# Two cross attentions, a linear and a low-rank attention, and a mixture of experts: outer products moved to VectorE, query evictions to ScalarE, fp16 halves in the last attention's projections, another turn in the routing

## The reference

```
x = x + L0_xattn(layernorm(x), ctx)   # queries Wq, keys Wk; values are ctx itself, scores / 32
x = x + L0_attn(layernorm(x))         # causal linear attention, 64 heads of 4:
        q, k = softmax(q), softmax(k)              # over the 4 of a head
        kv = cumsum(k (outer) v); kn = cumsum(k)   # over the rows
        out = (q . kv) / (q . kn), then Wo, bo
x = x + L0_ffn(layernorm(x))          # 3 cycles of a coupling net: gelu, gelu, gelu, sigmoid; twist
x = x + L1_xattn(layernorm(x), ctx)   # scores / 16, values ctx @ Wv + bv
x = x + L1_attn(layernorm(x))         # 16 heads of rank 64, value-output matrix 256x256 a head
x = x + L1_ffn(layernorm(x))          # attention over the 2 batches (4 heads), layernorm,
        # mixture of experts: gate of 8, argmax, at most 64 rows an expert in order of arrival;
        # h = rows @ w1 + b1 (1024), y = h @ w2 + b2, times the gate; layernorm
```

## Time and profile before

| | us |
|---|---|
| median of three runs (558.95 to 559.49) | 559.3 |
| the profiled execution | 559.52 |
| its span | 557.7 |
| TensorE busy (its granted clock: 0.995 of full speed) | 517.9 |
| VectorE, ScalarE, GpSimd busy | 355.6, 283.1, 76.5 |
| first cross attention and what it needs | 0 to 161 |
| between the cross attentions | 161 to 200 |
| second cross attention | 200 to 327 |
| low-rank attention | 327 to 475 |
| last attention | 475 to 500 |
| routing and experts | 500 to 558 |

### The profile page before, as it was taken

One profiled execution on the slowest core, in us unless ns is written; L12 is line 12 of the kernel. 1 busy time (PEld: TensorE's weight loads), 2 busy tenths in 40 slices (PEclk: granted clock), 3 DMA queues, 4 the chain that ended last, 5 costly groups with the idle time before them and its releaser, 6 DMA issues.

```text
span 557.7 us, 9466 instructions
## 1 busy us (share of the span) xinstructions
PE 517.9 (93%) x3588; PEld 357.5 (64%) x3588; DVE 355.6 (64%) x848; ACT 283.1 (51%) x616; POOL 76.5 (14%) x66
## 2 busy tenths in 40 slices
PE   8799998998999998999989999899999999988992
PEld 6565664555666654657545778788888778774551
DVE  4874646964547853356465647898888777654235
ACT  3777952627732038584266836898865444021110
POOL 0124131200011100000001320233301111200001
PEclk9999999999999999999999999999999999999998
DMA  8965570000000010000330040122158005960001
GB/s 270 307 208 102 115 160 29 1 2 1 1 0 1 1 29 0 2 1 0 109 118 2 2 152 2 39 78 77 39 164 351 1 1 183 350 223 1 1 1 38
DMA packets 45198, 44.06 MB, mean 79 GB/s; under 512 B 18657, under 2 KB 41185, under 8 KB 45025
## 3 DMA queue, kind: packets, MB, share of 16 engines
q1 hardware_dynamic: 45152, 43.45, 25.3%
HBM read 38.73 MB, written 0.52 MB: 70 GB/s over the span
## 4 chain that ended last, share of the span: by engine, by line
PE 65%; DVE 17%; issue 10%; ACT 6%; POOL 1%; DMA 1%; SPq 0%; DVEq 0%; ACTq 0%; POOLq 0%
PE ps L649 10%; PE ps L678 8%; PE ps L788 7%; PE ps L804 7%; PE ps L663 4%; PE ps L680 4%; PE ps L957 3%; PE ps L773 3%; PE ps L982 3%; PE ps L710 2%; PE ps L761 2%; PE ps L876 1%; DVE mx L1547 1%; ACT arena L1135 1%; ACT arena L1120 1%
## 5 line engine op out<-in xcount | busy, mean ns | idle before, releaser
L649 PE MATMUL ps<-ctx_tr,qtl 128*128 128x512 f16 x384 | 90.7, 379 | 2.1 <-ACT arena L1135 1.4
L1547 DVE TENSOR_REDUCE mx<-arena 128x1 f32<-128x512 f32 x64 | 43.1, 682 | 35.3 <-ACT arena L1135 34.6
L649 PEld LDWEIGHTS ps<-ctx_tr,qtl 128*128 128x128 f16 x384 | 36.7, 98 | 40.8 <-issue 3.2
L1135 ACT ACTIVATE arena<-ps 128x512 f32<-128x512 f32 x64 | 37.9, 595 | 43.9 <-PE ps L649 43.8
L678 PE MATMUL ps<-ctx_nat,pth 128*128 128x512 f16 x172 | 58.4, 379 | 0.0
L1120 ACT ACTIVATE arena<-arena,small 128x512 f32<-128x512 f32 x64 | 45.8, 716 | 6.3 <-DVE small L1556 6.3
L804 PE MATMUL ps<-arena,ctx_tr 128*128 128x256 f16 x384 | 47.2, 273 | 0.1
L680 PE MATMUL ps<-ctx_nat,ptl 128*128 128x256 f16 x172 | 46.9, 273 | 0.0
L663 PE MATMUL ps<-const,arena 128*128 128x128 f32 x256 | 39.1, 275 | 5.8 <-ACT arena L1120 5.1
L1561 DVE TENSOR_TENSOR ptl<-ps,pth 128x512 f16<-128x512 f32 x43 | 29.6, 688 | 21.6 <-ACT pth L1128 21.4
L1302 POOL TENSOR_TENSOR rstd<-mv,col 128x2 f32<-128x2 f32 x13 | 9.9, 765 | 239.4 <-DVE mv L1407 239.3
(11 more groups left out here) (294 smaller groups left out, 1037.9 us busy)
## 6 DMA issues: line engine op xcount, KB each, us to landing
ctx_nat<-in_w_e SPq DMA_DIRECT2D x8, 1024.0 KB, 7.7
ctx_tr<-in_w_e SPq DMA_DIRECT2D x6, 1024.0 KB, 11.6
...
```

Source lines behind the costliest of these rows:

```text
L649: mm = pe.matmul(ps[:, n % 2, :], qtl[:, qh, d, u * P:(u + 1) * P], CT[:, t0:t0 + KT, kh, d, :], start=(i == 0 and d == 0), stop=(i == 2 a ...
L1135: act.activation(S[:, n % SRING, :], ps[:, n % 2, :], ACT.Copy).then_inc(s("score_copied"), 1)
L1547: dve.tensor_reduce(mx[:, u, c:c + 1], S[:, n % SRING, :], AX.X, ALU.max).then_inc(s("score_max"), 1)
```

## The change

- Linear attention of batch 1: the two outer products go from GpSimd to VectorE, right behind the softmax of the keys. Those of batch 0 stay.
- `project("y", 0)`: the copy of the turned queries and the bias evictions of the projected ones go from VectorE to ScalarE.
- `BETWEEN`, `SIDE_AT`, `PREP_AT`, `LAST_AT`, `FILL`, `FILL_BETWEEN`: other numbers.
- Last attention, tiles 0 to 2: `w6i` is cut into fp16 halves `w6h` (1536 elements a partition, the high half by ScalarE, the low half by VectorE), the turned latents into `x6h`, and the projections are three fp16 products instead of one fp32. Tile 3 is as before. `w6i` has a semaphore of its own.
- Routing: the rows of the first pair of experts are gathered first (columns 0 to 127, banks 2 and 3), then the others (384 columns, banks 6 and 7); the two evictions no longer wait for one another. `Sm` is turned behind `hidden(0)` (banks 4 to 7) instead of before, and its copies follow the evictions of `hidden(0)`.
- `combine(g)` does the products with the high half of all four tiles first and waits for the low half after them.

```diff
@@ -65,12 +65,12 @@
 LA_WAIT = 4
-FILL = (18, 6, 43, 0, 34)
+FILL = (21, 3, 40, 0, 31)
 FILL_TURN = 5
 LAST_AT = (
-    (49, 50, 51, 54, 55, 58, 59, 62, 70, 71,),
-    (65, 70,),
-    (43, 47, 48, 48, 50, 52, 54, 55, 55, 56, 57, 60, 62, 64, 67, 69,),
+    (49, 51, 53, 54, 55, 58, 59, 64, 69, 71,),
+    (40, 48, 57, 66, 70,),
+    (42, 44, 46, 48, 49, 52, 52, 54, 55, 55, 56, 57, 59, 64, 65, 67, 69,),
 )
@@ -118,47 +118,47 @@
-PREP_AT = [0, 1, 2, 3, 4, 5, 6, 7, 9, 13, 15, 23, 25, 28, 31]
+PREP_AT = [0, 1, 2, 3, 4, 5, 6, 7, 9, 15, 16, 23, 25, 28, 31]
         (
-            (67, 67, 69, 69, 69, 69, 70, 71, 76, 81, 84, 88, 88, 90, 92, 95, 97, 100, 102, 103, 104, 105, 105, 114, 118,
+            (66, 67, 68, 69, 69, 72, 73, 76, 77, 81, 87, 89, 89, 92, 93, 95, 97, 100, 102, 103, 104, 105, 105, 110, 114,
              120, 121, 122, 123, 127,),
-            (63, 67, 68, 68, 68, 72, 72, 73, 75, 89, 93, 93, 93, 93, 94, 94, 99, 102, 103, 105, 105, 105, 105, 114, 118,
-             120, 121, 121, 122, 123, 124,),
-            (64, 65, 65, 67, 69, 69, 69, 71, 71, 80, 81, 84, 87, 89, 91, 95, 97, 97, 99, 101, 103, 104, 105, 115, 117,
-             121, 124, 124, 125, 125,),
+            (63, 64, 68, 68, 68, 74, 75, 76, 78, 89, 93, 93, 94, 94, 96, 96, 99, 102, 104, 105, 105, 105, 105, 114, 114,
+             121, 121, 122, 122, 123, 124,),
+            (64, 65, 65, 67, 68, 72, 72, 75, 77, 80, 82, 85, 88, 89, 91, 93, 97, 97, 97, 100, 103, 104, 105, 111, 117,
+             123, 124, 124, 124, 125,),
         ),
...
         (
-            (4, 8, 11, 13, 14, 15, 17, 18, 23, 24, 25, 26, 30, 30, 32, 33, 34, 35, 40, 45, 46, 50, 51, 53, 54, 56, 57,
-             58,),
-            (3, 3, 5, 13, 14, 15, 16, 18, 23, 23, 23, 24, 24, 28, 30, 33, 34, 40, 45, 49, 52, 53, 53, 55, 59, 59, 61,
+            (3, 9, 9, 10, 13, 14, 17, 19, 23, 25, 26, 27, 29, 30, 32, 33, 35, 36, 40, 43, 44, 50, 51, 53, 54, 56, 60,
+             60,),
+            (1, 3, 5, 9, 13, 14, 17, 18, 23, 23, 24, 26, 27, 29, 31, 33, 35, 40, 44, 46, 49, 52, 52, 55, 59, 60, 62,
              62,),
-            (3, 4, 8, 10, 10, 12, 16, 18, 20, 21, 23, 24, 26, 27, 28, 30, 31, 34, 43, 45, 47, 49, 51, 53, 55, 56, 58,
-             59,),
+            (1, 4, 6, 8, 10, 10, 17, 18, 20, 21, 24, 26, 26, 28, 30, 30, 33, 34, 42, 45, 47, 49, 51, 53, 57, 60, 63,
+             63,),
         ),
...
 BETWEEN = (
-    "aayyayaaaayyyayaaayayyayya",
-    "aaaayayayyaayyayayyayaaa",
-    "yaaaayyayaayayyayayaayaaa",
+    "ayayayaaayyayaaayayayyayya",
+    "ayaaayaayyyyaaayyayyyaa",
+    "yaaaayaayyayayyayayaayaaa",
 )
@@ -179,7 +179,8 @@
-FILL_BETWEEN = {0: 8, 3: 6, 11: 52, 12: 6, 13: 16, 20: 8}
+FIRST_PAIR, OTHERS = (2, slice(0, 2 * CAP)), (6, slice(2 * CAP, E6 * CAP))
+FILL_BETWEEN = {0: 8, 3: 6, 11: 52, 12: 6, 13: 16, 20: 13}
@@ -322,6 +323,8 @@
         b1c = wts[:, 3856:3920].rearrange("p (e f) -> p e f", e=E6)
+        w6h = ctx_tr[:, 10752:12288].bitcast(F16).rearrange("p (h c n) -> p h c n", h=2, c=DC)
+        x6h = wts[:, 2048:2816].bitcast(F16).rearrange("p (h c n) -> p h c n", h=2, c=DC)
@@ -336,6 +339,7 @@
         ys = rest[:, 0:256]
+        turned_places = lambda g: ps[:, 4 + g, 0:SEQ].bitcast(F16)
             pe.wait_ge(s("m_qkv0"), n)
+        pe.wait_ge(s("w6_lo"), 1)
         for c in range(DC):
-            mm = pe.matmul(ps[:, 6, 0:cols[1] - cols[0]], x0T[:, c, t * P:(t + 1) * P], w6i[:, c, cols[0]:cols[1]],
-                           start=(c == 0), stop=(c == DC - 1))
+            for k, (xh, wh) in enumerate(((0, 0), (0, 1), (1, 0))):
+                mm = pe.matmul(ps[:, 6, 0:cols[1] - cols[0]], x6h[:, xh, c, t * P:(t + 1) * P],
+                               w6h[:, wh, c, cols[0]:cols[1]], start=(c == 0 and k == 0), stop=(c == DC - 1 and k == 2))
         mm.then_inc(s("m_qkv0_ps"), 1)
@@ -927,29 +934,33 @@
     pe.wait_ge(s("id16"), 1)
-    for t in range(NT):
-        pe.wait_ge(s("m_S"), t + 1)
-        for c in range(DC):
-            for h in range(2):
-                mm = pe.matmul(ps[:, c, :], y1[:, h, t, c * P:(c + 1) * P], Sm[:, t, :], start=(t == 0 and h == 0),
-                               stop=(t == NT - 1 and h == 1))
-            if t == NT - 1:
-                mm.then_inc(s("m_dis_ps"), 1)
-    for g in range(E6 // 2):
-        to = ps[:, 2 + g, 0:SEQ].bitcast(F16)
+    for to, cols in FIRST_PAIR, OTHERS:
         for t in range(NT):
-            mm = pe.transpose(to[:, t * P:(t + 1) * P], Sm[:, t, g * P:(g + 1) * P], id16)
-        mm.then_inc(s("m_ST_ps"), 1)
+            pe.wait_ge(s("m_S"), t + 1)
+            for c in range(DC):
+                for h in range(2):
+                    mm = pe.matmul(ps[:, to + c, cols], y1[:, h, t, c * P:(c + 1) * P], Sm[:, t, cols],
+                                   start=(t == 0 and h == 0), stop=(t == NT - 1 and h == 1), skip_group_check=True)
+                if t == NT - 1:
+                    mm.then_inc(s("m_dis_ps"), 1)
+
+    def turn_places():
+        pe.wait_ge(s("m_dis0"), 2)
+        pe.wait_ge(s("m_dis1"), 2)
+        for g in range(E6 // 2):
+            for t in range(NT):
+                mm = pe.transpose(turned_places(g)[:, t * P:(t + 1) * P], Sm[:, t, g * P:(g + 1) * P], id16)
+            mm.then_inc(s("m_ST_ps"), 1)
...
-        if g == 0:
-            pe.wait_ge(s("m_dis"), 2)
-        else:
+        if g < 2:
+            pe.wait_ge(s("m_dis0"), g + 1)
+            pe.wait_ge(s("m_dis1"), g + 1)
+        if g:
             pe.wait_ge(s("m_h"), 2 * g)
         pair = (2 * g, 2 * g + 1)
         for f in range(2):
         pe.wait_ge(s("m_h"), 2 * g + 2)
-        if g == 0:
-            pe.wait_ge(s("m_ST"), 4)
-        else:
+        if g:
             pe.wait_ge(s("m_hT"), 2 * g)
@@ -971,6 +980,8 @@
             pe.wait_ge(s("m_y"), g)
+        else:
+            pe.wait_ge(s("m_ST"), 4)
         pair = (2 * g, 2 * g + 1)
@@ -984,18 +995,19 @@
     def combine(g):
-        pe.wait_ge(s("m_y"), g + 1)
-        for b in range(B):
-            for t in (2 * b, 2 * b + 1):
-                for h in range(2):
+        for h in range(2):
+            pe.wait_ge(s("m_y_hi" if h == 0 else "m_y"), g + 1)
+            for b in range(B):
+                for t in (2 * b, 2 * b + 1):
                     mm = pe.matmul(ps[:, 6 + b, (t % 2) * D:(t % 2 + 1) * D], ST[:, g, t * P:(t + 1) * P], yy[:, g, h],
...
                                    skip_group_check=True)
-            if g == E6 // 2 - 1:
-                mm.then_inc(s("m_comb"), 1)
+                if g == E6 // 2 - 1 and h == 1:
+                    mm.then_inc(s("m_comb"), 1)
...
     hidden(0)
+    turn_places()
     for g in range(G):
@@ -1031,7 +1043,17 @@
     yield
-    yield
+    if (what, b) == ("y", 0):
+        act.wait_ge(s("xn_turned"), NORM[what, b] + 1)
+        act.activation(xnT_of(what, b), bank(side_banks(what, b)[0], a=DC), ACT.Copy).then_inc(s("xnT"), 1)
+    yield
+    if (what, b) == ("y", 0):
+        act.wait_ge(s("px_q"), k + 1)
+        act.wait_ge(s("px_qt"), k)
+        for e in range(DC):
+            q = act.activation(qT_of(what, b)[:, e, :], ps[:, side_banks(what)[1], e * SEQ:(e + 1) * SEQ], ACT.Identity,
+                               bias=C("%s_bq%d" % (what, e)))
+        q.then_inc(s("qT"), 1)
     yield
@@ -1211,7 +1233,7 @@
-    early = leave_pair(0, 6)
+    early = enter_last()
     for n in late(-1):
@@ -1231,6 +1253,22 @@
+            def enter_last():
+    def latents_hi(k, tiles, n):
+        act.wait_ge(s("xn_turned"), NORM["m", k] + 1)
+        w = len(tiles) * P
+        act.activation(x6h[:, 0, :, tiles[0] * P:tiles[0] * P + w], ps[:, n, 0:2 * w].rearrange("p (c n) -> p c n", c=DC),
+                       ACT.Copy).then_inc(s("m_x_hi"), 1)
+
+    act.wait_ge(s("w6i_in"), 16)
+    act.activation(w6h[:, 0], w6i, ACT.Copy).then_inc(s("w6_hi"), 1)
+    yield
+    latents_hi(0, (0, 1), 6)
+    yield
+    latents_hi(1, (2,), 6)
+    yield
+    yield from leave_pair(0, 6)
+
             def leave_pair(j, b_turn):
     act.activation(e8, e8, ACT.Exp).then_inc(s("m_exp8"), 1)
-    act.wait_ge(s("m_dis_ps"), 1)
-    act.activation(disT[:, 0, :], ps[:, 0, :], ACT.Copy).then_inc(s("m_dis"), 1)
-    for g in (0, 2):
+    for k, (at, cols) in enumerate((FIRST_PAIR, OTHERS)):
+        act.wait_ge(s("m_dis_ps"), 2 * k + 1)
+        act.activation(disT[:, 0, cols], ps[:, at, cols], ACT.Copy).then_inc(s("m_dis0"), 1)
+
+    def places(g):
         act.wait_ge(s("m_ST_ps"), g + 1)
-        act.activation(ST[:, g, :], ps[:, 2 + g, 0:SEQ].bitcast(F16), ACT.Copy).then_inc(s("m_ST"), 1)
+        act.activation(ST[:, g, :], turned_places(g), ACT.Copy).then_inc(s("m_ST"), 1)
+
     for g in range(E6 // 2):
@@ -1270,6 +1311,9 @@
             y_hi(g - 1)
+        else:
+            places(0)
     y_hi(E6 // 2 - 1)
             layernorm("y", 0)
+        if b:
+            continue
         pool.wait_ge(s("a_soft"), n + 1)
@@ -1425,14 +1471,16 @@
     yield
-    turned(what, b)
-    yield
-    dve.wait_ge(s("px_q"), k + 1)
```

(44 more changed lines are left out.)

19 lines of the change are left out of this document (10 added, 9 removed), and 6 rows, old and new, of the table SIDE_AT.

## The result

| us | before | after |
|---|---|---|
| median of 11 runs | 559.49 (558.95 to 560.68) | 557.47 (556.07 to 559.13) |
| profiled execution | 559.52, span 557.7 | 558.75, span 557.0 |

The ratio is 0.9956, 95% interval 0.9946 to 0.9967: 2.5 us faster on 559.49, between 1.8 and 3.0 (the two medians differ by 2.0). The forecast was 557.0 and "faster".

The account below looks back on a forecast made before the run. Bounds: TensorE in the low-rank stage, VectorE between the attentions, a relay from routing on. Terms -0.35-1.0-0.75-0.2, lists 0, sum to -2.3 on 559.52: 557.2 profiled, 557.0 median; range 555.0 to 559.0 (forecast's own 556.2 to 558.1).

Parts of the forecast that it names:

- Part 1: Between the cross attentions: the chain and the next attention's first scores come 0.35 us earlier; from -0.98 to +1.2.
- account of the stall, -1.85: Between the attentions: VectorE's twist takes 2.33 us beside GpSimd's product, 0.48 without; the move saves 1.85.
- +0.59 for them up to the queries: Between the attentions: VectorE's added outer products, 2.44, less the stall, 1.85, up to batch 0's normalised queries.
- +0.59 for the place: Between the attentions: by the shared-port rule against moving work, the place gives +0.59 us, not -0.35.
- Part 2: Low-rank stage, last attention's projections in fp16 halves: 1.94 us saved, 0.9 lost, so -1.0; from -1.94-0.4 to +0.4.
- the step that binds: Low-rank stage, step 23: VectorE's 1.75 us load minus 0.6 falls on 0.96 of slack; 0.2 to 0.8 of stall.
- the price put on top: Low-rank stage: stall up to 0.8 us at step 23 and 0.3 each at steps 24 and 25; 1.1 in all.
- rival (a): Low-rank stage: VectorE absorbs the weights' low half, TensorE gets 1.94 and the exposed loads; -1.3 more, 555.7; chance 0.20.
- Part 3: Routing: experts start at 508.0 instead of 508.75, transposes hidden; -0.75 us, from -0.9 to -0.3.
- Part 4: Last combine: four products go during the 0.52 us wait for the low half; -0.2 us, from -0.4 to 0.
- Part 5: Lists of the two cross attentions: waits move, nothing gained; 0 us, from -1.0 to +1.0.
- Rival (c): Second cross attention: the feed-forward's early Gelu delays the row maxima; up to +5 us on the forecast, 562.0; chance 0.11.

Follow-up runs that it names:

- e9: Kernel after with batch 1's outer products back on GpSimd and 8 instead of 13 dummy products ahead of the queries' turn; median 556.19 us, ratio to before 0.9942.
- e1: Kernel before with only the fp16 halves of the last attention's projections added; median 557.84 us, ratio to before 0.9982.
- e6: Kernel after with the subtraction that makes the weights' low halves done twice; median 558.61 us, ratio to before 0.9984.
- e3: Kernel before with only the routing and last-combine edits added; median 559.13 us, ratio to before 0.9997.
- e4: Kernel before with only the new lists of the two cross attentions (PREP_AT, SIDE_AT); median 559.88 us, ratio to before 1.0007.

## Why the prediction was right, and where its steps were off

| part | forecast | own trace | in after |
|---|---|---|---|
| 1 between the attentions | -0.35 | -0.37 and -0.27 later | -0.40 |
| 5 lists | 0 | +0.33 | with the -0.27: +0.02 |
| 2 halves | -1.0 | -1.85 | -1.85 |
| 3 routing | -0.75 | -0.66 | -0.67 |
| 4 combine | -0.2 | -0.22 | -0.22 |
| sum | -2.3 | -3.04 | -3.12 |

The direction and the sizes of parts 1, 3 and 4 were right. That the time came within 0.5 us of the forecast is in part luck, since two differences of opposite sign met: by the traces the edits gave 0.8 more than foreseen, and the run times show 0.6 less of it than the traces.

**Part 1** was right in size, and in what bounds it (the query product, then TensorE's sums, with VectorE waiting 0.49). Its account of the stall, -1.85, was right too. What it did not draw from its own working is that the outer products gain nothing in it: the working has +0.59 for them up to the queries, 0.4 with the gaps taken off (measured 0.29), and e9 shows 0.27 lost. The rule that moving work between these two engines might not help (the Trainium skill, Perfetto Trace Analysis, "Optimizing Scalar/DVE Operations") is borne out by that 0.27; the whole part is still a gain, so the prediction's +0.59 for the place did not come.

**Part 2** is the term that was mis-sized: -1.0 forecast, -1.85 measured. Its first half, the 1.94 saved by the products, was right: from the first start of each piece to what follows it, the six pieces take 8.12 us in before and 6.15 in e1, 1.97 less. So was the working for the step that binds, 1.75 less 0.6 that VectorE regains less 0.96 of slack, 0.2 of stall at step 23: in e1 VectorE is 1.67 us late (its start taken off) at the subtraction for step 22 and 1.22 at that for step 23, and TensorE waits 0.16 there. What failed is the price put on top: 0.8 as that step's upper value, "and 0.3 more each at steps 24 and 25", for which no row was read. Behind the subtraction for step 24 before has 1.98 us of slack; e1 has 0.29 left there, and no wait in that step or the next. "I take 1.1 us in all" was 0.16. TensorE's idle time in the stage was to rise from 0.6 to 1.5; it is 0.52 (117.00-116.48) after 0.57. So rival (a) is what happened, VectorE took the load, short of (a)'s size: of its 2.3 us the 0.4 for exposed loads of weights did not come (around the pieces' own products lie 0.35 us in before and 0.31 in e1). One reading was wrong without effect: the residual and the casts stand a half-step later in after (44) than in before (43), not earlier; both are ahead of the same subtraction. e6 shows how near the limit it was: the next 1.81 us cost 1.79.

**Part 3** fell short by 0.08: TensorE's 32 products of both ranges took 4.09 us to their modelled end, where the forecast took 2.6 for the second range; the experts waited for these and for nothing else. That the transposes are hidden was right: TensorE's pause there fell from 1.49 to 0.49. **Part 4** was right.

**Part 5** was right for the first attention: the pause of 1.39 went, and in its place TensorE waits 0.35 and 1.14 behind the products that follow, 1.49 for the 1.7 foreseen. In the second the lists cost 0.33. Rival (c) did not come: the first exponential is 0.97 us late in after, 0.92 before.

**From 3.1 to 2.5.** Most run times fall into groups, 556.1 to 556.6 and 557.3 to 557.9 for after, 559.0 to 559.5 and 560.3 to 560.7 for before; three of the 22 lie outside. The distance, 1.2 to 1.4 us, is that of one fall of the clock (1.27 at 490 us); that the upper groups are such falls is likely, but a run time has no trace to show it. Lowest against lowest is 558.95-556.07 = 2.9. More of after's runs lie more than 1 us above their lowest (7 of 11, 4 of 11 before), and that takes the rest from the median. Whether after is more prone to it stays open: its fewer dummies in the last attention leave a pause of 0.59 us at 487.6 where before has 0.27, but e3 and e4 fell with before's numbers. Also open: the ratios of most of the single parts are 0.1 to 0.9 us less favourable than their traces.
